# Result made from SBUF in each block, no reloads; layer weights in parts; one sine operation per q or k; residual sum between the rotations

## The reference

```python
x = x + 0.5 * ffn(layernorm(x))          # stack 0: DEPTH = 2 layers
x = x + attn(layernorm(x))               # full attention over 1024 tokens, plus its own residual
x = x + 0.5 * ffn(layernorm(x))          # stack 1: the same weights

def layer(x):                            # inside ffn
    h = shift_token(x)                   # upper 64 features come from the token before
    q, k, v = split(h @ wqkv)            # 8 heads of 64
    q = l2norm(q) * qs; k = l2norm(k) * ks
    q, k = rotary_xpos(q, k)             # q*cos + rotate_half(q)*sin, with a scale
    o = local_attention(q, k, v)         # windows of 64, each with the window before
    x = x + o @ wo
    h = layernorm(shift_token(x)) * g + b
    a, g = split(h @ w1 + b1)
    return x + (a * gelu(g)) @ w2 + b2
```

## Time and profile before

| | |
|---|---|
| median of 3 runs | 1751.31 us (1747.47 to 1751.98) |
| the profiled execution | 1754.54 us, its span 1752.7 us |
| granted TensorE clock, mean | 0.967 |
| TensorE busy (matmul) | 1540.5 us, 88% |
| VectorE busy | 1366.0 us, 78% |
| ScalarE busy | 1172.7 us, 67% |
| GpSimd busy | 1091.5 us, 62% |
| DMA | 112.44 MB, 64 GB/s |

### The profile page before, as it was taken

How to read it: one execution, slowest core, us unless ns; L and a number is a source line. 1 busy time by engine, 2 the same in 40 slices (tenths; PEclk the granted TensorE clock), 3 DMA queues, 4 the chain that set the end, 5 groups by cost and what they waited for, 6 DMA issues and landing times.

```text
span 1752.7 us, 43881 instructions
## 1 busy us (share of the span) xinstructions
PE 1540.5 (88%) x15864; PEld 1241.5 (71%) x15864; DVE 1366.0 (78%) x3516; ACT 1172.7 (67%) x2364; POOL 1091.5 (62%) x1106
## 2 busy tenths in 40 slices
PE   1889999979999999877889889999998999999974
PEld 1677777767878777755666667777776777777763
DVE  6678888878797979757776479797977797979763
ACT  1577777767777777733455478786866686878761
POOL 3676768667676777612333178585856586868550
PEclk9999999999999999978999989999998999999996
DMA  8231212232312131113100142121222222212104
GB/s 286 55 120 42 61 44 63 52 97 48 77 44 57 43 82 41 41 30 124 37 25 13 43 109 55 45 55 46 64 59 83 73 53 51 55 47 54 46 21 121
DMA packets 183670, 112.44 MB, mean 64 GB/s; under 512 B 86721, under 2 KB 164129, under 8 KB 182945
## 3 DMA queue, kind: packets, MB, share of 16 engines
q1 hardware_dynamic: 183456, 109.65, 24.0%
HBM read 43.41 MB, written 23.42 MB: 38 GB/s over the span
## 4 chain that ended last, share of the span: by engine, by line
PE 65%; DVE 14%; ACT 7%; issue 6%; SPq 4%; DMA 2%; POOL 1%; DVEq 0%; ACTq 0%; POOLq 0%
PE QK L389 14%; PE TO L639 9%; PE TO L758 6%; PE SC L680 6%; PE TO L724 5%; PE QK L639 4%; PE TO L389 4%; PE VB L389 4%; ACT probs L1309 3%; PE SC L662 2%; PE TO L809 2%; PE VB L809 2%; PE VB L639 2%; PE TO L919 2%; DVE rope_s L1166 2%
## 5 line engine op out<-in xcount | busy, mean ns | idle before, releaser
L1490 POOL TENSOR_TENSOR rnorm<-clip,mhalf 128x8 f32<-128x8 f32 x128 | 210.1, 1641 | 310.6 <-DVE clip L1122 310.5
L1309 ACT ACTIVATE probs<-SC,shift,qgain 128x128 f32<-128x128 f32 x1024 | 371.3, 481 | 0.2
L389 PE MATMUL QK<-w_qkv,hT 128*128 128x512 f32 x768 | 218.5, 421 | 49.2 <-issue 15.9
L1509 POOL TENSOR_TENSOR qgain<-clip,mhalf 128x8 f32<-128x8 f32 x128 | 211.3, 1651 | 0.0
L389 PEld LDWEIGHTS QK<-w_qkv,hT 128*128 128x128 f32 x768 | 139.9, 196 | 97.2 <-issue 52.7
L1303 ACT ACTIVATE pT<-TO 128x1024 f32<-128x1024 f32 x160 | 163.7, 1023 | 48.9 <-PE TO L639 48.9
L1099 DVE TENSOR_REDUCE top<-SC 128x4 f32<-128x512 f32 x256 | 174.9, 683 | 20.5 <-PE SC L680 18.1
L1166 DVE TENSOR_TENSOR rope_s<-QK,rope 128x256 f32<-128x256 f32 x512 | 190.8, 414 | 0.0
L639 PE MATMUL TO<-ident,probs 128*128 128x128 f32 x1280 | 174.0, 276 | 9.0 <-ACT probs L1309 5.3
L639 PEld LDWEIGHTS TO<-ident,probs 128*128 128x128 f32 x1280 | 150.9, 142 | 42.8 <-issue 22.5
L1161 DVE TENSOR_TENSOR rope_c<-QK,rope 128x512 f32<-128x512 f32 x256 | 173.2, 676 | 9.8 <-PE QK L389 9.5
(11 more groups left out here) (174 smaller groups left out, 3447.7 us busy)
## 6 DMA issues: line engine op xcount, KB each, us to landing
v_prev<-v_own SPq DMA_DIRECT2D x256, 130.0 KB, 2.3
x_att<-stream SPq DMA_DIRECT2D x128, 64.0 KB, 2.3
h<-stream SPq DMA_DIRECT2D x256, 32.0 KB, 1.9
stream<-x_new SPq DMA_DIRECT2D x32, 256.0 KB
w_qkv<-qkv_d SPq DMA_DIRECT2D x3, 1536.0 KB, 6.5
h<-x_mid SPq DMA_DIRECT2D x128, 32.0 KB
h<-x_mid SPq DMA_DIRECT2D x128, 31.8 KB
rope<-rope_d SPq DMA_DIRECT2D x24, 128.0 KB, 3.1
```

Of the source, the lines that this page charges most:

```text
L389: last = mm(dst, fr(left(a)), fr(right(b)), start=(k == 0), stop=(k == 2))
L1309: last = nc.scalar.activation(probs[:, b, hd, :], SC[:, hd * P:hd * P + P], ACT.Exp, bias=shift[:, b, hd:hd + 1], scale=qgain[:, b, hd % 4 ...
L1490: g.tensor_tensor(rnorm[:, b, :], clip2[:, b, 8:16], mhalf[:, 0:8], ALU.pow).then_inc(s_rn, 1)
L1509: g.tensor_tensor(qgain[:, b, :], clip2[:, b, 0:8], mhalf[:, 0:8], ALU.pow).then_inc(s_qg, 1)
```

## The change

1. Result. In stack 1, layer 1 (the last), VectorE makes the result from x_new in SBUF (`finished`): for sequences 0 to 2 whole, in the burst that follows; for sequence 3 in halves, right behind each half of x_new. SyncE stores it to `out` (`result`) in place of the store to `stream`. `kept` is (v_g, pT2, x_2, x_2b); for sequences 2 and 3 the attention's result stays where it was made, so only two are stored to `mid` and reloaded. The store, reload and sum at the end are gone.
2. Weights. `w_o` holds both layers, loaded once at the start. `w_qkv` is loaded in two parts: q and k after `s_k` of the last tile, v after `s_v`, with a semaphore of its own (`s_vw`).
3. The sine product is one operation of 128x512 for q and one for k; it reads the halves of each head in reverse order.
4. Order on VectorE: bn_stats, clip, bn_aggr, rotation of q, x_mid, rotation of k.

```diff
-        w_o = sb("w_o", [P, PAIRS, DIM])
+        w_o = sb("w_o", [P, DEPTH, PAIRS, DIM])
-        kept = (v_g, x_2, pT2, pT)
-        half_step = (x_att, x_mid, x_b2, sq)
+        kept = (v_g, pT2, x_2, x_2b)

-            def load_qkv(l):
-                sp.dma_start(w_qkv[:], qkv_d[l]).then_inc(s_qkvw, 16)
-            def load_wo(l):
-                sp.dma_start(w_o[:], wo_in[l].rearrange("(c p) n -> p c n", p=P)).then_inc(s_wow, 16)
+            def load_qk(l):
+                sp.dma_start(w_qkv[:, :, 0:1024], qkv_d[l, :, :, 0:1024]).then_inc(s_qkvw, 16)
+            def load_v(l):
+                sp.dma_start(w_qkv[:, :, 1024:1536], qkv_d[l, :, :, 1024:1536]).then_inc(s_vw, 16)
+            def result(s):
+                sp.wait_ge(g_x2, ROWS + s + 1)
+                sp.dma_start(rows(out[s]), tokens(kept[s])).then_inc(g_out, 16)
...
                             lb, sb_ = divmod(n - 1, SEQS)
-                            store(lb, sb_, n - 1 + first)
+                            if k == 0 or lb == 0:
+                                store(lb, sb_, n - 1 + first)
+                            elif sb_ > 0:
+                                result(sb_ - 1)
...
                 if k == 0:
-                    load_wo(0)
+                    sp.dma_start(w_o[:], wo_in.rearrange("l (c p) n -> p l c n", p=P)).then_inc(s_wow, 16)
...
-                    for s in range(SEQS - 1):
+                    for s in range(2):
                         sp.wait_ge(g_mid[s], 16)
                         sp.dma_start(tokens(kept[s]), rows(mid[s])).then_inc(g_fin[s], 16)
...
-                def after_qkv():
+                def after_qk():
+                    wait_tile(s_k, m + TILES - 1)
+                    load_qk(1)
+                def after_v():
                     wait_tile(s_v, m + TILES - 1)
-                    load_qkv(1)
-                def after_wo():
-                    wait_tile(s_y, m + TILES - 1)
-                    load_wo(1)
+                    load_v(1)
-                iteration(SEQS, [(0, rope_after(5)), (1, rope_after(6)), (2, after_qkv), (2, rope_after(7)), (6, after_wo)],
+                iteration(SEQS, [(0, rope_after(5)), (1, rope_after(6)), (2, after_qk), (2, after_v), (2, rope_after(7))],
...
             stack(1)
-            stack_done(sp, 1)
-            sp.dma_start(tokens(kept[SEQS - 1]), rows(mid[SEQS - 1])).then_inc(g_fin[SEQS - 1], 16)
-            for s in range(SEQS):
-                sp.dma_start(tokens(half_step[s]), rows(stream[DEPTH, s, 1:, :])).then_inc(g_fin[s], 16)
-            for s in range(SEQS):
-                sp.wait_ge(g_x2, ROWS + s + 1)
-                sp.dma_start(rows(out[s]), tokens(kept[s])).then_inc(g_out, 16)
+            result(SEQS - 2)
+            for half in range(2):
+                sp.wait_ge(g_x2, ROWS + SEQS + half)
+                a, b = half * HALF, (half + 1) * HALF
+                sp.dma_start(rows(out[SEQS - 1, a * P:b * P, :]), tokens(kept[SEQS - 1])[:, a:b, :]).then_inc(g_out, 16)
...
+            def rotated(t, m, signal):
+                i = t.i
+                dve.wait_ge(signal, t.count())
+                src = qk(QK[:, :])[:, m]
+                v.tensor_tensor(qk(rope_c[:])[:, m], src,
+                                rope[:, i, m, 0:1, :].to_broadcast([P, HEADS, DH]), ALU.mult)
+                sin = rope[:, i, m, 1:2, :].rearrange("p o (a d) -> p o a d", a=2)
+                last = v.tensor_tensor(qk(rope_s[:])[:, m].rearrange("p h (a d) -> p h a d", a=2),
+                                       src.rearrange("p h (a d) -> p h a d", a=2)[:, :, ::-1, :],
+                                       sin.to_broadcast([P, HEADS, 2, 32]), ALU.mult)
+                return last
+            def finished(s, t):
+                v.scalar_tensor_tensor(out=tokens(kept[s])[:, t, :], in0=x_new[:, t, :], scalar=0.5,
+                                       in1=tokens(kept[s])[:, t, :], op0=ALU.mult, op1=ALU.add).then_inc(g_x2, 1)
...
+                        if before == 2 * ITERS - 1:
+                            dve.wait_ge(s_xn, before * 2 + (half + 1))
+                            finished(SEQS - 1, slice(half * HALF, half * HALF + HALF))
-                if t := tile(QKV + 1):
-                    clipped(t)
                 if t := tile(FFN_IN):
                     b, k = t.i % 2, t.i % 4
                     dve.wait_ge(s_h2[k], t.count(every=4, unit=48))
                     v.bn_stats(st2[:, b, :], h2[:, k, :]).then_inc(s_st2, 1)
+                if t := tile(QKV + 1):
+                    clipped(t)
+                if t := tile(FFN_IN):
+                    dve.wait_ge(s_st2, t.count())
+                    v.bn_aggr(mv2[:, t.i % 2, :], st2[:, t.i % 2, :]).then_inc(s_mv2, 1)
+                if t := tile(QKV):
+                    dve.wait_ge(s_rope[t.i], t.loads() * 16 - 15)
+                    need(dve, s_qr, t.count(back=1))
+                    need(dve, s_ka, t.count(back=1))
+                    rotated(t, 0, s_q)
                 if t := tile(WO):
                     i = t.i
                     dve.wait_ge(s_y, t.count())
...
                     v.tensor_tensor(x_mid[:, i, :], OB[:, 0:DIM], x_att[:, i, :], ALU.add).then_inc(s_xm, 1)
-                if t := tile(FFN_IN):
-                    dve.wait_ge(s_st2, t.count())
-                    v.bn_aggr(mv2[:, t.i % 2, :], st2[:, t.i % 2, :]).then_inc(s_mv2, 1)
                 if t := tile(QKV):
...
-                        sin = rope[:, i, m, 1:2, :]
-                        for half in range(2):
-                            a, o = 32 * half, 32 * (1 - half)
-                            last = v.tensor_tensor(qk(rope_s[:])[:, m, :, a:a + 32], src[:, :, o:o + 32],
-                                                   sin[:, :, a:a + 32].to_broadcast([P, HEADS, 32]), ALU.mult)
-                    last.then_inc(s_rot, 1)
+                    rotated(t, 1, s_k).then_inc(s_rot, 1)
...
+                    if (s := n - ITERS - SEQS - 1) >= 0:   
+                        if s < 2:
+                            dve.wait_ge(g_fin[s], 16)
+                        dve.wait_ge(s_xn, n * 2)
+                        finished(s, slice(0, TILES))
```

More of the change, by code:

```diff
@@ L230, in build @@
         s_qkvw = sem("s_qkvw")
+        s_vw = sem("s_vw")
         s_wow = sem("s_wow")
@@ L288, in build @@
         g_in = sems("g_in", SEQS)
-        g_fin = sems("g_fin", SEQS)
+        g_fin = sems("g_fin", 2)
         g_st = sem("g_st")
@@ L329, in build @@
         g_on = sem("g_on")
-        g_mid = sems("g_mid", SEQS)
+        g_mid = sems("g_mid", 2)
         g_new = sems("g_new", SEQS)
@@ L510, in iteration @@
                         if j == 0 and l > 0:
-                            need(sp, s_st, (first - 1 + n) * 32 + 16)
+                            need(sp, s_st, (first - 1 + (min(n, SEQS + 1) if k else n)) * 32 + 16)
                         if j == 0 and l == 0 and k == 1:
@@ L594, in stack @@
                     sp.dma_start(x_h1, rows(stream[DEPTH, 1, 1:, :])).then_inc(g_ld, 16)
-                store(1, SEQS - 1, first + ITERS - 1)
+                    store(1, SEQS - 1, first + ITERS - 1)
             stack(0)
@@ L607, in attention_stores @@
                 sp.wait_ge(g_x2, (s + 1) * TILES)
-                sp.dma_start(rows(mid[s]), x_o[s % 2][:]).then_inc(g_mid[s], 16)
+                if s < 2:
+                    sp.dma_start(rows(mid[s]), x_o[s % 2][:]).then_inc(g_mid[s], 16)
                 sp.wait_ge(g_on, s + 1)
                 sp.dma_start(rows(stream[0, s, 1:, :]), x_new[:]).then_inc(g_new[s], 16)
-            load_qkv(0)
-            load_wo(0)
+            load_qk(0)
+            load_v(0)
             for i in range(TILES):
@@ L719, in f @@
                     if t := tile(WO):
-                        if t.i == 0:
-                            pe.wait_ge(s_wow, t.loads() * 16)
+                        if t.c == 0:
+                            pe.wait_ge(s_wow, 16)
                         pe.wait_ge(s_oT, t.count())
                         for c in range(PAIRS):
-                            last = mm(OB[:, 0:DIM], oT[:, c, :], w_o[:, c, :], start=(c == 0), stop=(c == PAIRS - 1))
+                            last = mm(OB[:, 0:DIM], oT[:, c, :], w_o[:, t.c // TILES // SEQS, c, :], start=(c == 0), stop=(c == PAIRS - 1))
                         last.then_inc(s_y, 1)
@@ L731, in f @@
                             pe.wait_ge(s_xn, before * 2 + 1)
+                        if t.i == 0:
+                            need(pe, s_vw, (t.loads() - 1) * 16)
                         product(mm, VB[:], lambda x: hT[:, b, x, :], lambda x: w_qkv[:, x, 1024:1536]).then_inc(s_v, 1)
@@ L1133, in step @@
                             dve.wait_ge(s_xb2, tile(FFN_IN + 1).count())
-                            dve.wait_ge(s_st, before * 32 + 16)
+                            if before > ITERS + SEQS:
+                                dve.wait_ge(g_x2, ROWS + before - ITERS - SEQS)
```

(24 more changed lines are left out.)

5 lines of the change are left out of this document (3 added, 2 removed).

## The result

The changed kernel took 1720.32 us (median of 3 runs, 1719.33 to 1725.11) against 1751.31: ratio 0.9836, 95% interval 0.980 to 0.9872, so 31 us faster. A second measurement, on the chip of the first four experiments, gave 1725.0 against 1750.57, ratio 0.9858 (0.9838 to 0.9879), 26 us. The forecast was 1725, within 1710 to 1735.

A forecast was written before the change was run, and what follows sets the result against it. The prediction took a loop of norm, clip, GpSimd's chain to k_a and a held shift as the bound, not TensorE. Its terms, -15.4 - 5.4 - 3.2 - 10.4 - 1.5 + 9.8 = -26.1 us, gave 1725, within 1710 to 1735.

The forecast's parts named there:

- Tail: From the last x_new to the span's end: 18.9 us becomes 3.2 plus 0.3 of backlog, -15.4 us.
- w_o: At the layer changes: both layers stay in SBUF, so TensorE's two waits for w_o go, -5.4 us.
- w_qkv in parts: At the two layer changes: the smaller q and k load lands in 4.85 us, not 6.5, -3.2 us.
- The tile after a burst: In 14 tiles behind feed-forward bursts: earlier q_r and k_a release the shift 0.74 us sooner each, -10.4 us.
- The tiles behind w_qkv's wait: Two tiles with the same chain of product, rotations, scores and shift: -0.75 us each, -1.5 us.
- bn_stats ahead of clip: In the loop on VectorE: clip starts 0.10 us later, seven times in each of 14 sequences, +9.8 us.
- Sine product: On VectorE: one operation for two spares a start, but h2n is ready before k_r ends anyway, worth 0.
- x_mid's delay: On VectorE: x_mid comes some 1.2 us later but its readers need it later still, cost 0.
- A: Rival: the second shift gets the port before k_a, TensorE's 8.67 us becomes the step, -31, 1694 us; 8%.
- B: Rival: bn_stats costs its whole 0.20 us (+10), or the shift behind a burst stays held (+10), 1735 us; 12%.
- C: Rival: bn_stats waits for late copies and holds clip and GpSimd in every tile; 0.5 us each gives 1772; 3%.
- D: Rival: weights late (+3.2 us) and store backlog at the end (+1.9), 1730 us; 10%.

The follow-up runs named there:

- the first four experiments: e1 to e4, run on one chip, where the changed kernel took 1725.0 us against 1750.57 for the kernel before.
- e3: The changed kernel with clip ahead of bn_stats again: 1713.39 us, ratio 0.9782 to the kernel before.
- e4: e3 with norm moved ahead of the second shift, in a burst too: 1720.87 us, ratio 0.9829 to the kernel before.
- e8: e4 with one wait more, GpSimd's q_r waiting for the first shift of the same step: 1699.23 us, ratio 0.9712 to the kernel before.
- e11: The changed kernel with clip ahead of bn_stats and q_r waiting for the first shift, norm still behind the second shift: 1717.9 us, ratio 0.9798.
- e5: The kernel before with only point 1 of the change, the result made from SBUF: 1738.01 us against 1749.64, ratio 0.9929.
- e7: The changed kernel with one layer of w_o in SBUF, reloaded at the change of layer: 1725.67 us, ratio 0.9856 to the kernel before.
- e6: The changed kernel with w_qkv loaded in one piece after s_v, w_o still resident: 1720.98 us.
- e2: The changed kernel with x_mid back ahead of both rotations: 1735.77 us, ratio 0.9912 to the kernel before.
- e9: The changed kernel with the sine product in two halves again, for q and for k: 1721.63 us, ratio 0.9805 to the kernel before.
- e1: The changed kernel run once more, unaltered, as yardstick: 1725.0 us.
- e10: e8 with bn_stats ahead of clip, as in the changed kernel: 1700.11 us, ratio 0.9699 to the kernel before.
- e12: e8 with both parts of w_qkv loaded one step earlier in SyncE's order, ahead of the last tile's v_prev copies: 1688.32 us against 1753.56.

## Why the prediction was right, and by how much each step

**The bound: right.** e3, e4, e8 and e11 show a loop of norm, clip, GpSimd to k_a and a held shift; TensorE becomes the bound at 8.67 throughout only when the loop is open and the first shift is kept free (e8).

**Tail, -15.4: right.** 19.00 became 3.47, and the three whole results cost nothing that shows. e5's time gives it as 10 to 15.

**w_o, -5.4: 5.6 to 7.1.** In the kernel before, the two stretches into a burst with this wait are 23.55 and 22.70, where the others are 20.3: 5.6 together, as forecast. In the changed kernel the same reload costs 7.1 (e7). I weighed 1 us of slow products against 1 us of catching up; there the slow products weighed more.

**w_qkv in parts, -3.2: 0.1 to 0.5** (e6). The bound "0" was in the text, for another reason (both parts sharing the engines). The transfer got 0.9 and 1.0 shorter and not 1.65, and the step left out TensorE's clock behind the wait, which gave back 1.2 and 0.4. The section "Anatomy of one DMA" of the Trainium skill's page "DMA: Bandwidth & Descriptors", whose fit the prediction sets beside this term, states it for DMAs that GpSimd issues; SyncE issues these, and they took 5.47 and 6.46, not the 4.4 and 5.6 of that estimate.

**The tile after a burst, -10.4: right.** The forecast let the shift go at 1575.68, 7.77 behind its clip; measured, 7.78 (1553.03 to 1560.81). Its stretch to the next rnorm shrank by 0.88, and e2 puts 0.76 of it on x_mid's place. **The tiles behind w_qkv's wait, -1.5: somewhat more.** Over the wait the kernel before has 16.83 and 17.79 from rnorm to rnorm, e6, which loads in one piece as well, 15.90 and 16.44: 2.3 in two tiles. The shift there is free now (0.19 and 0.16, from 1.25 and 0.53). No run changes the order alone at this place.

**bn_stats ahead of clip, +9.8: the step that was sized too high.** The way to a plain tile's rnorm grew by 0.07 and not by 0.10 (8.96 to 9.03), six times a sequence. Summed over one sequence, the forecast was six plain tiles at +0.10, the stretch into the burst at +0.20 (counted in the term of the tile behind it) and that tile at -0.94 + 0.10: -0.04. Measured: +0.4 in the six tiles, +0.2 and -0.88, so -0.3, and over the plain pairs -0.38. Over 14 sequences the difference makes some 4 us. e3 takes this order back alone: 0.6 a sequence, 14 x 0.6 = 8.4.

**Sine product 0: right** (e9). **x_mid's delay 0: right:** plain tiles of e2 and e1 are equal, 9.03.

The table of stretches gives -15.5 for the tail, -8.0 for the two changes of layer (9.4 without their four sequences' 1.4) and 14 x -0.35 = -4.9 for the sequences: -28.4 of the 29.4. The forecast had -15.4, -10.1 (w_o, w_qkv and the tiles behind it) and -0.6 (-10.4 + 9.8), -26.1. So the main mechanisms were right, but that the sum came so close is in part luck: 2 us too much at the change of layer stand against 4 too little in the sequences.

**Rivals.** A, that the second shift comes first, didn't happen: it starts 0.02 us behind k_a (e1 to e3). A meeting this close does change the time: in e4 the first shift met q_r and was held. A's price was also added up wrongly: its three parts (1.5, 0.7 and 0.7) make 2.9 a sequence and not 2.2. With the loop open e8 and e10 gain 1.5 a sequence. By the Trainium skill's page "SBUF — State Buffer", section "SBUF: two separate sides", whichever of the two starts first has the ports to its end. The traces agree but for the closest meetings: every shift that starts with q_r or k_a or up to 0.06 us behind is held (1.29 behind k_a in the changed kernel), and in e8, where the order is forced and it starts 0.33 ahead, it takes 0.17. Within 0.02 us ahead they don't tell who was first: the shift of e4 shown above starts 0.02 ahead of q_r by the trace and is held 1.30, and of e4's 41 shifts that start 0.01 or 0.02 ahead 15 were held and 26 were free. The page counts a two-input VectorE operation among those that need the pair; norm, with one input, ran beside k_a unheld (1.21), which agrees too. B would have asked for a shift of 1.26 behind the burst: it is 0.51. C, that bn_stats waits for its copies, came true in single tiles only: three waits, 7.5 us in all, against two and 5.7 before. One of them, 0.40 at 450.17, stands ahead of the clip behind the burst after the first change of layer, and that tile takes 11.61 in place of 11.13 (e3, with clip first: 11.11). Of D nothing was seen: no v product waits for its weights, and the end, 3.47, is as forecast (18.9 - 15.4).

## What to carry to other kernels

Look for short operations with a long duration: they are waits that no view names, and they can close a loop between two engines that both look idle. Put work that needs no shared port beside the other engine's work, and then check where the next two-input operation meets it: an open loop only moves the meeting, and a wait of 0.2 us on the right side is cheaper than a hold of 1.3. Weigh a load by when it leaves its queue before its size, and count the slow products behind a wait of TensorE with the wait.

## What the runs showed of the hardware that I had not expected

- A wait costs TensorE more than its length: behind the w_qkv wait its six q and k products took 2.93 us in place of 1.63, at a granted clock of 0.50, and shortening the wait by 1.0 us at the second change left the stretch at half clock 0.9 longer, which gave back 0.4; at the first more came back than was saved (e6).
- The fall can come after the wait: in e7 the clock was still 1.00 in the stretch where w_o arrived and 0.50 from 1363.0, more than a microsecond into the products behind it (from 1361.73).
- A small copy behind a large load suffers: the last `h<-x_mid` of a tile landed 5.85 us after its issue began, behind 1.5 MB of weights (e12), and the issue alone took 3.59; in the changed kernel's chain of waits in the first sequence such a copy has 2.92.
